# Attention products with V placed directly behind the last scores, one slot earlier

## What is computed

```
scores = jnp.einsum('bld,blwd->blw', q, kw) / scale     # 15 neighbours of each token
attn = jax.nn.softmax(scores, axis=-1)
out = jnp.einsum('blw,blwd->bld', attn, vw)             # the products with V
...
x = shortcut + h
m = jax.nn.gelu(m @ fc1_w + fc1_b, approximate=False) @ fc2_w + fc2_b
...
main = jax.nn.gelu(x @ W1m + b1m) @ W2m + b2m
h = jax.nn.gelu(jnp.einsum('bnd,bkdh->bknh', x, W1g) + b1g[:, :, None, :])
eo = jnp.einsum('bknh,bkhd->bknd', h, W2g) + b2g[:, :, None, :]
expert_out = jnp.einsum('bk,bknd->bnd', gate_w, eo)
return a * main + (1.0 - a) * expert_out
```

## Time and profile before

| what | value |
|---|---|
| median of 3 runs | 1879.69 us (1879.02 to 1880.44) |
| the profiled execution, its own time | 1879.39 us |
| its span, first to last instruction | 1877.6 us |
| TensorE, VectorE, ScalarE, GpSimd busy | 1865.5, 1358.6, 1169.2, 872.1 us |
| mean granted TensorE clock | 1.000 |

### The profile page before, as it was taken

One profiled execution on the slowest core, in us unless ns is written; L12 is line 12 of the kernel. 1 busy time (PEld: TensorE's weight loads), 2 busy tenths in 40 slices (PEclk: granted clock), 3 DMA queues, 4 the chain that ended last, 5 costly groups with the idle time before them and its releaser, 6 DMA issues.

```text
span 1877.6 us, 49306 instructions
## 1 busy us (share of the span) xinstructions
PE 1865.5 (99%) x19591; PEld 1684.6 (90%) x19591; DVE 1358.6 (72%) x2230; ACT 1169.2 (62%) x1832; POOL 872.1 (46%) x788
## 2 busy tenths in 40 slices
PE   8999999999999999999999999999999999999999
PEld 7899898998989989899898999989899898998998
DVE  7776877778677686776867767687676877778644
ACT  5775755657566575665756657566575755657554
POOL 6545271543716436163462524536245271552725
PEclk9999999999999999999999999999999999999999
DMA  5230311203122031220313103131131311203121
GB/s 143 63 90 29 97 58 53 73 29 96 57 68 68 19 102 52 83 60 24 97 46 91 52 30 96 41 96 53 38 89 34 97 58 49 77 29 97 46 63 57
DMA packets 147438, 121.88 MB, mean 65 GB/s; under 512 B 17965, under 2 KB 140041, under 8 KB 147209
## 3 DMA queue, kind: packets, MB, share of 16 engines
q1 hardware_dynamic: 146512, 117.90, 21.9%
q10 hardware_dynamic: 696, 0.83, 0.2%
HBM read 85.52 MB, written 8.39 MB: 50 GB/s over the span
## 4 chain that ended last, share of the span: by engine, by line
PE 97%; DVE 1%; DMA 1%; ACT 0%; POOL 0%; issue 0%; ACTq 0%; DVEq 0%; POOLq 0%
PE psB L253 58%; PE psA L253 28%; PE psA L1266 4%; PE psA L1283 3%; PE psA L1155 2%; PE psA L1305 2%; PE psA L1321 0%; DMA raw<-in_L_attn_qkv_w 0%; DMA raw<-in_L_attn_fc_w 0%; DVE smax L726 0%; POOL y L520 0%; DMA xin<-in_L_attn_x 0%; PE psB L1340 0%; ACT y L1019 0%; DVE pr L743 0%
## 5 line engine op out<-in xcount | busy, mean ns | idle before, releaser
L626 DVE TENSOR_TENSOR hr_lo<-hf,hr_hi 128x512 fp32r<-128x512 f32 x512 | 495.5, 968 | 435.8 <-ACT hr_hi L982 435.8
L514 POOL TENSOR_SCALAR wx_hi<-raw 128x512 fp32r<-128x512 f32 x256 | 196.6, 768 | 658.6 <-DMA raw<-in_L_ffn_W2e 387.7
L982 ACT ACTIVATE hr_hi<-hf 128x512 fp32r<-128x512 f32 x512 | 324.2, 633 | 276.0 <-PE psB L253 187.9
L516 POOL TENSOR_TENSOR wx_lo<-raw,wx_hi 128x512 fp32r<-128x512 f32 x256 | 410.8, 1605 | 21.4
L978 ACT ACTIVATE hf<-psB,b1x 128x512 f32<-128x512 f32 x256 | 175.4, 685 | 178.2 <-PE psB L253 177.0
L253 PE MATMUL psB<-wx_hi,hr_hi 128*128 128x256 f32 x1016 | 285.2, 281 | 0.2
L253 PE MATMUL psB<-wx_hi,hr_lo 128*128 128x256 f32 x1016 | 284.1, 280 | 0.0
L253 PE MATMUL psB<-wx_lo,hr_hi 128*128 128x256 f32 x1016 | 283.5, 279 | 0.0
L253 PE MATMUL psB<-z_hi,wx_hi 128*128 128x512 f32 x512 | 211.8, 414 | 0.0
L253 PE MATMUL psB<-z_hi,wx_lo 128*128 128x512 f32 x512 | 202.5, 396 | 0.0
L253 PE MATMUL psB<-z_lo,wx_hi 128*128 128x512 f32 x512 | 201.1, 393 | 0.0
(11 more groups left out here) (213 smaller groups left out, 4643.9 us busy)
## 6 DMA issues: line engine op xcount, KB each, us to landing
raw<-in_L_ffn_W1e SPq DMA_DIRECT2D x256, 128.0 KB, 2.2
raw<-in_L_ffn_W2e SPq DMA_DIRECT2D x256, 128.0 KB, 2.2
vb<-vs SPq DMA_DIRECT2D x64, 192.0 KB
vb<-vs SPq DMA_DIRECT2D x64, 160.0 KB
out_x<-acc SPq DMA_DIRECT2D x31, 256.0 KB, 2.2
xin<-in_L_attn_x SPq DMA_DIRECT2D x15, 512.0 KB, 3.7
tm<-in_L_ffn_b2e SPq DMA_DIRECT2D x32, 128.0 KB, 3.0
raw<-in_L_attn_fc_w SPq DMA_DIRECT2D x8, 256.0 KB, 3.5
```

Of the source, the lines that this page charges most:

```text
L514: g.tensor_scalar(wx[0][:, s, :], raw[:, s, :], 1.0, 0.0, ALU.mult, ALU.add).then_inc(w_hi.sem, 1)
L516: g.tensor_tensor(wx[1][:, s, :], raw[:, s, :], wx[0][:, s, :].bitcast(f32), ALU.subtract).then_inc(w_lo.sem, 1)
L626: v.tensor_tensor(hr[1][:, c % 2, :], hf[:, c % 3, :], hr[0][:, c % 2, :].bitcast(f32), ALU.subtract).then_inc(h_lo.sem, 1)
L982: a.activation(hr[0][:, c % 2, :], hf[:, c % 3, :], ACT.Copy).then_inc(h_hi.sem, 1)
```

## The change

In rows 1 to 15 the products with V of units 0 and 1 come directly behind the scores of unit 3 in slot 7. In slot 8 of those rows only up(8) and down(6) are left. So TensorE's order goes from scores, up(8), down(6), products with V to scores, products with V, up(8), down(6). Row 0 keeps its order, and the other engines' programs are the same.

```diff
--- before.py
+++ after.py
@@ -1412,12 +1412,12 @@
                     elif q == 7:
                         if t:
                             scores(t, 3)
+                            attend(t, 0)
+                            attend(t, 1)
                         else:
                             attend(t, 0)
                             turn(t, 2)
-                    elif q == 8:
-                        if t:
-                            attend(t, 0)
+                    elif q == 8 and t == 0:
                         attend(t, 1)
                     elif q == 10:
                         turn(t, 2 if t else 3)
```

## The result

| | before | after |
|---|---|---|
| median (range) | 1879.71 us (1879.02 to 1880.44) | 1915.66 us (1913.21 to 1918.34) |
| the profiled execution | 1879.39 us | 1913.21 us |
| its span | 1877.6 us | 1911.3 us |

The ratio is 1.0192, 95% interval 1.0178 to 1.0205: the change makes the kernel 36 us slower. I had forecast slower by 21, with a range up to 1908.

What follows compares the result with a forecast made beforehand. TensorE was taken as the bound, busy 1865.5 of 1877.6 us. To 1879.4 came 4.0 (late chain net of changes of kind) and 18 (instruction supply): 1901 us predicted, range 1884 to 1908.

Steps and rivals of the forecast that it cites:

- Term 3: Joined scores and products with V use up 256-instruction blocks before the next arrives; TensorE stalls, +18 us (bounds 10 to 26).
- three classes of rows: Rows 1 to 15 by block border, about 56, 140 or 224 instructions behind unit 3's scores: 10, 8 and no us.
- class at 56: Rows 2, 5, 8, 11, 14, border about 56 instructions into unit 3's scores: stalls of 2.0 us each, 10 us.
- class at 140: Rows 3, 6, 9, 12, 15, border at the start of the products with V: stalls 0.8 to 2.2, together 8 us.
- Term 2: hr_hi(8), held by down(6), starts 0.55 us later; down(9) waits 0.40; net of Term 1 +0.27 a row, +4.0 us.
- Term 1: Fewer changes of matmul kind on TensorE: 0.13 us a row saved (0.31 if scores to V is cheap), -2.0 us.
- no shortage of instructions: Rival: no instruction stalls, only Term 2 costs: 1883.4 us (bound 1880.8); chance 12%.
- faster: Rival: scores to products with V costs nothing, blocks never late, h_low(9) keeps up: 4.6 us saved, 1874.8; chance 6%.

Runs made afterwards that it cites:

- experiment 5: Changed kernel, 21 of unit 2's score calls issued twice, 92 instructions added at the start, block border about 56 behind unit 3's scores in every row: 1932.06 us.
- Experiment 2: Changed kernel with the GELU table loaded early on ScalarE, behind exp of unit 2 in slot 7: 1910.80 us, ratio 1.0158.
- experiment 1: Kernel before with only down(6) moved behind the products with V in slot 8, the scores staying in slot 7: 1894.17 us, ratio 1.0075.
- experiment 8: GELU table loaded early in two kernels: changed one with doubled score calls and border at 232 (1897.02 us); one with only unit 0's products moved (1881.24 us).
- Experiment 7: Changed kernel with VectorE's last operation of unit 2's normalisation put behind the gather in rows 1 to 15: 1922.09 us, ratio 1.022.
- experiment 4: Changed kernel with 84 instructions of tiny matmuls and loads added at the very start, moving the block borders: 1912.51 us, ratio 1.0176.
- experiment 6: Changed kernel, 21 of unit 2's score calls issued twice, 172 instructions added at the start, border about 232 behind unit 3's scores: 1905.77 us, ratio 1.0139.

## Why the prediction was wrong

**Term 3, the supply of instructions, was right in kind, place and nearly in size.** 18 us forecast, 15.8 in the profile. The blocks of 256, the borders counted from row 0's two gaps and the three classes of rows held. In the profile after and in experiment 5, TensorE goes on 1.2 to 1.6 us after the end of the transfer in each gap from row 1 on, and in the ten gaps of the profile after the next block could be used 2.9 to 3.8 us after the border before it, 3.3 on average, where I had 3.5. The gaps of the class at 56 were 9.6 us against 10. Those of the class at 140 came 1.8 short: there it was 3.2 on average, and the gap of row 3 cost nothing. The figure holds for bursts alone: in the kernel before, by the same count, the blocks of rows 3 and 6 last 2.5 and 3.0 us, and no gap follows. As forecast, rows 1, 4, 7, 10 and 13 have none. The page "Runtime: NRT & Kernel Launch" of the Trainium skill, section "Instruction fetch mechanics", gives TensorE room for 2,048 instructions; these runs do not agree with that, since a burst of 384 instructions with a border near its start runs it dry (15 gaps in experiment 5). They fit the two lines of 16 KiB in the same section.

**Term 2 is the step that failed.** I wrote that "gelu(8) is no part of it: up(8) would end at 460.03, and ScalarE is held to 460.24 by its table load". That took the table load as done before ScalarE waits for up(8). The load stands behind the wait: in the earlier trace rows it started at 458.94, when exp was done, because up(8) had ended by then. Moving up(8) by 1.27 us put the load behind its new end, and the delay of hr_hi(8) was 1.10 us, not 0.55. Experiment 2 took the load out of the way: the delay was 0.52, and 0.66 us a row came back.

**Term 2 also missed who waits first.** I took down(9), with 0.35 us of slack, as the first to be late. It is down(8): it starts a new sum in the PSUM banks that the gather reads, and two lines of chunk_down say so (a cut from its conditions):

```
elif j == 0 and m:
    pe.wait_ge(acc_s.sem, acc_s.at(t - 1, 2 * (m // KH - 1) + h))
```

Its slack against the late chain was 0.35 as well: hr_hi(8) late by 1.10, 0.72 and 0.52 (the change, experiments 1 and 2) puts down(8) 0.75, 0.37 and 0.17 later behind the start of the scores than before, each time 0.35 less. So this oversight changed the place and hardly the price: with nearly my delay, a row of experiment 2 is 0.32 longer than before, where the prediction had 0.27. Of the 10.5 us that terms 1 and 2 are off, the table load is 9 to 10 (15 times the 0.59 to 0.66 that experiments 8 and 2 give back), and all the rest under 2. Experiment 7 shows both waits on one chain. A third buffer of hr, which would free hr_hi(8) from down(6), was not tried.

**Term 1** is inside its bounds of 0.13 and 0.31 us a row: 0.21 was saved. I took the dear bound because the change of shape looked like the entries that are seen, and it is cheaper.

**The clock.** "I charge no loss of clock for stalls of 2 us" was wrong. The granted clock fell to 1.2 GHz for 3.4 us shortly behind the gaps of rows 2, 5, 8 and 15, not behind those of rows 11, 12 and 14; in row 5 matmuls of 512 columns then have a pitch of 0.43 us in place of 0.23. About 1.7 us is lost each time (3.4 us at half the clock), and part of it comes back in rows 2, 5 and 15, where down(8) then waits 0.23 us or not at all for the gather; in row 8 it still waits 0.78. With the border at 56 it fell in only 2 of 15 rows with gaps of like length. What decides it stays open. The spread of the change's six times (1913 to 1918, against 1.4 us before) is what differing numbers of falls would give; that is argued, not shown.

Of the rivals, "no shortage of instructions" falls with experiments 4 to 6, "faster" with all of them. The measured time lies outside the range because both errors, the chain's 10.5 us and the clock's 4, went the same way, and only the supply's 2 the other.

## What to carry to other kernels

Instructions are data too: where short matmuls stand together, count them in blocks from a gap put down to issue, and ask how long a block lasts against the time that its successor's transfer needs; an edit far away can move such a gap by changing the count. When TensorE is full and an operation is put ahead of a chunk, follow that chunk through each engine to every wait of TensorE on it, and take a table load as part of the operation behind its wait, not as cover for it.

## What the hardware showed that I had not expected

- The same program with 80 more tiny instructions at the start is 26 us faster, 1905.77 for 1932.06.
- Stalls of 1.6 to 2.3 us on TensorE were followed by 3.4 us at 1.2 GHz in some rows and not in others with the same gap.
- A run of small matmuls with another tile shape starts 1.07 us after the start of the scores, no later than a large matmul does (1.08), though behind large matmuls the step to it takes 0.21 us.
- VectorE's multiply with a broadcast took 2.07 us in 11 rows in which it started within 0.05 us of a GpSimd operation of 1.30 us, for 0.95 us a few steps earlier in the same row.
